# A scatter's wait moved ahead of the next scatter, and a one-hot table laid out with its tiles innermost

## The reference

```
sig = sigmoid(x @ Wg.T);  topk_idx = top_k(sig + e_bias, 6)         # 6 of 128 experts per token
topk_w = 2.5 * sig[topk_idx] / sum(sig[topk_idx])
# per expert a list of at most 192 (CAP) tokens with their weights
g, u = split(x[tokens_of_e] @ W_gate_up[e]);  y = (silu(g) * u) @ W_down[e] * weight
out = x_in;  out[tokens_of_e] += y;  out += (silu(x @ Wsg) * (x @ Wsu)) @ Wsd
```

## Time and profile before

| | |
|---|---|
| median of 3 runs | 946.81 us (944.99 to 950.73) |
| the profiled execution | 954.78 us, span 953.0 us |
| TensorE (PE) busy | 846.6 us, 89% |
| VectorE (DVE) busy | 750.6 us, 79% |
| ScalarE (ACT) busy | 343.4 us, 36% |
| GpSimd (POOL) busy | 308.2 us, 32% |
| last chain, by engine | DVE 41%, PE 28%, issue 11%, POOL 7%, DMA 7% |

### The profile page before, as it was taken

How to read it: one execution, slowest core, us unless ns; L and a number is a source line. 1 busy time by engine, 2 the same in 40 slices (tenths; PEclk the granted TensorE clock), 3 DMA queues, 4 the chain that set the end, 5 groups by cost and what they waited for, 6 DMA issues and landing times.

```text
span 953.0 us, 22207 instructions
## 1 busy us (share of the span) xinstructions
PE 846.6 (89%) x7603; PEld 766.5 (80%) x7603; DVE 750.6 (79%) x3738; ACT 343.4 (36%) x971; POOL 308.2 (32%) x350
## 2 busy tenths in 40 slices
PE   1787899899899899899899999998999999999993
PEld 1676688788798788788799999988878878878782
DVE  4256899999899899899999896988635666676662
ACT  0325554553553554544544435331100222122220
POOL 6021212412412312312313311031102556656564
PEclk8799999999999999999999999999986999999997
DMA  7410010110001001001101000001104455565541
GB/s 204 127 51 1 2 35 16 37 32 21 29 20 33 29 17 35 30 17 35 29 19 35 26 20 27 25 25 41 45 5 112 115 143 147 128 152 142 128 115 29
DMA packets 48663, 54.25 MB, mean 57 GB/s; under 512 B 8981, under 2 KB 41595, under 8 KB 48540
## 3 DMA queue, kind: packets, MB, share of 16 engines
q1 hardware_dynamic: 39372, 44.23, 16.3%
q0 software_dynamic: 6592, 7.28, 4.8%
q10 hardware_dynamic: 2608, 1.60, 0.7%
HBM read 42.40 MB, written 10.69 MB: 56 GB/s over the span
## 4 chain that ended last, share of the span: by engine, by line
DVE 41%; PE 28%; issue 11%; POOL 7%; DMA 7%; ACT 3%; SPq 2%; DVEq 0%; POOLq 0%; ACTq 0%
DVE b_arena L1497 10%; POOL b_arena L1758 4%; DMA out_rows<-b_hid,b_add_index 3%; POOL out_rows L1788 3%; DMA out_rows<-b_inner,b_add_index 3%; DVE b_top_a L1483 3%; PE p_big L685 3%; PE p_big L686 2%; DVE b_top_d L1483 2%; PE p_shared L830 2%; DVE b_top_c L1483 2%; PE p_shared L831 2%; DVE b_top_b L1483 2%; DVE b_rstd L1235 2%; PE p_small L866 2%
## 5 line engine op out<-in xcount | busy, mean ns | idle before, releaser
L1758 POOL DMA_INDIRECT b_arena<-x_rows,b_index x44 | 75.0, 1705 | 103.4 <-issue 66.3
L1541 DVE TENSOR_TENSOR b_arena<-b_iota_b,b_slot 128x1152 bf16<-128x1152 bf16 (+1 forms) x46 | 85.2, 1855 | 15.0 <-issue 15.0
L685 PE MATMUL p_big<-b_xT,b_ff1a 128*128 128x128 f32 x384 | 77.7, 285 | 1.4 <-ACT b_xT L1025 1.4
L686 PE MATMUL p_big<-b_xT,b_ff1b 128*128 128x128 f32 x384 | 76.9, 283 | 0.0
L1692 POOL TENSOR_TENSOR b_arena<-b_kY,b_mask_k 64x256 f32<-64x256 f32 x16 | 9.8, 611 | 204.8 <-ACT b_kY L1050 204.8
L1025 ACT COPY b_xT<-p_small 128x256 f32<-128x256 f32 (+1 forms) x97 | 35.5, 377 | 83.2 <-PE p_small L676 83.1
L1723 POOL TENSOR_TENSOR b_arena<-b_arena 128x768 f32<-128x768 f32 x16 | 27.0, 1690 | 117.6 <-DVE b_arena L1509 117.6
L685 PEld LDWEIGHTS p_big<-b_xT,b_ff1a 128*128 128x128 f32 x384 | 61.8, 200 | 2.5 <-ACT b_xT L1025 2.5
L686 PEld LDWEIGHTS p_big<-b_xT,b_ff1b 128*128 128x128 f32 x384 | 61.1, 200 | 0.0
L996 PE MATMUL p_big<-b_xeT,b_arena 128*116 128x192 f32 x320 | 60.1, 331 | 0.0
L719 PE MATMUL p_big<-b_arena,b_q_blk 128*128 128x256 f32 (+3 forms) x256 | 48.9, 334 | 12.4 <-ACT b_q_blk L1057 12.4
(11 more groups left out here) (367 smaller groups left out, 2589.6 us busy)
## 6 DMA issues: line engine op xcount, KB each, us to landing
b_arena<-in_w_gate_up SPq DMA_DIRECT2D x20, 464.0 KB
b_arena<-in_w_down SPq DMA_DIRECT2D x20, 336.0 KB
b_xp<-in_xp SPq DMA_DIRECT2D x16, 384.0 KB, 3.1
b_arena<-in_w_gate_up SPq DMA_DIRECT2D x40, 116.0 KB
xT_rows<-b_xmT SPq DMA_DIRECT2D x16, 128.0 KB, 1.8
b_xT_late<-xT_rows SPq DMA_DIRECT2D x16, 128.0 KB, 2.2
h_rows<-b_h SPq DMA_DIRECT2D x16, 96.0 KB, 1.6
x_rows<-b_xm SPq DMA_DIRECT2D x32, 48.0 KB, 2.0
```

Of the source, the lines that this page charges most:

```text
L685: mm(o, ff1a[:, c * 128:(c + 1) * 128], xTa[s][:], start=True, stop=False)
L686: last = mm(o, ff1b[:, c * 128:(c + 1) * 128], xTb[s][:], start=False, stop=True)
L1541: last = tt(hot[s][:, tiles, :], iota_b[:, None, :].to_broadcast([128, n, CAP]), slot[:, tiles, bass.ds(e, 1)].to_broadcast([128, n, CAP]) ...
L1758: G.indirect_dma_start(xg[s][:, h, :], None, x_rows[:, :], bass.IndirectOffsetOnAxis(index[s][:, h:h + 1], 0)).then_inc(S(f"gathered{s}"), 16)
```

## The change

`hot` is laid out with the 192 places outside and the tiles inside, 18 of them so that the number is even (`NTP`; the last is never used), and `slot` likewise with the experts outside and the tiles inside. The constants 1 to 192 are kept repeated 18 times (`iota_t`). All operands of the comparison then have innermost steps of one element. The comparison is made in two operations of 96 places, both behind the two silu products; TensorE takes the 96 weights of a load 18 elements apart. GpSimd counts `add_done` and issues the scatter after a wait for the scatter before, instead of waiting behind its own; the zero rows' two transfers move from SyncE's queue to GpSimd's and count on the semaphore `added`.

```
@@ -31,9 +31,9 @@
 DX = D + DB
 HS = CAP // 2
 NT = TILES + 1
+NTP = NT + 1
 DUMMY = T
 ROWS = T + CAP
-HOT_FIRST = 6
 AHEAD = 4
 LATE = 9
 LIST = E + 4
@@ -310,7 +310,7 @@
 
 
 SEMAPHORES = """
-    h3_kept0 h3_kept1 xT_kept0 xT_kept1 fetched0 fetched1 at0_T at1_T at0_aT at1_aT zero_rows x_stored
+    h3_kept0 h3_kept1 xT_kept0 xT_kept1 fetched0 fetched1 at0_T at1_T at0_aT at1_aT x_stored
     acc_stored0 acc_stored1 patch_mm xm_ready acc_ready c_xm_ready cls_x_stored  cls_acc_stored list_ready
     eup1 down_mm w_loaded0 w_loaded1 h0_ready h0_T ff0_xT ff0_up ff0_hid
     ff0_down y_ready y_T at0_xT at0_qk at0_v at0_k_sb at0_four at0_qk_sb at0_s
@@ -399,7 +399,7 @@
         cls_before_f = arena[1][0:B, 512:512 + TILES * 128]
         pat_before_f = arena[1][:, 0:TILES * B]
         iota_f = sb("iota_f", [128, CAP + 1])
-        iota_b = sb("iota_b", [128, CAP], bf16)
+        iota_t = sb("iota_t", [128, CAP, NTP], bf16)
         tok_f = sb("tok_f", [128, NT * 3])
         dummy_f = sb("dummy_f", [HS, 2])
         eval_f = sb("eval_f", [128, 2])
@@ -493,7 +493,7 @@
         chosen = sb("chosen", [128, NT, E], bf16)
         before_sum = sb("before_sum", [128, NT, E], bf16)
         wsplit = sb("wsplit", [128, NT, E + 1, 3], bf16)
-        slot = sb("slot", [128, NT, E + 1], bf16)
+        slot = sb("slot", [128, E + 1, NTP], bf16)
         counts, active_f = sb("counts", [128, 1]), sb("active_f", [128, 1])
         active = sb("active", [128, 1], bf16)
         rank, pick = sb("rank", [128, 1]), sb("pick", [128, LIST], bf16)
@@ -501,7 +501,7 @@
         n_pairs = sb("n_pairs", [1, 1])
 
 
-        hot, at = carve(0, 128, NT, CAP, dt=bf16)
+        hot, at = carve(0, 128, CAP, NTP, dt=bf16)
         rhs = two("rhs", [128, NT, 6], bf16)
         slot_a, slot_b = two("slot_a", [HS, 2]), two("slot_b", [HS, 2])
         slot_w, add_w = two("slot_w", [HS, 2]), two("add_w", [HS, 2])
@@ -607,8 +607,6 @@
                     sp.wait_ge(presets, 1)
                 for dst, src in group:
                     sp.dma_start(dst, src).then_inc(done, 16)
-            sp.dma_start(x_rows[T:ROWS, :].rearrange("(p r) d -> p (r d)", r=2), zrows[:]).then_inc(S("zero_rows"), 16)
-            sp.dma_start(out[T:ROWS, :].rearrange("(p r) d -> p (r d)", r=2), zrows[:, 0:2 * D]).then_inc(S("zero_rows"), 16)
 
             sp.sem_inc(S("x_stored"), 64)
 
@@ -924,7 +922,7 @@
                 pe.wait_ge(S("hot_ready"), v)
                 for h in range(2):
                     for t in range(NT):
-                        last = mm(lists_bank[s][0:HS, 400 + 6 * h:406 + 6 * h], hot[s][:, t, h * HS:(h + 1) * HS], rhs[s][:, t, :],
+                        last = mm(lists_bank[s][0:HS, 400 + 6 * h:406 + 6 * h], hot[s][:, h * HS:(h + 1) * HS, t], rhs[s][:, t, :],
                                   start=(t == 0), stop=(t == NT - 1))
                 last.then_inc(S("index_mm"), 1)
 
@@ -1407,7 +1405,7 @@
                 yield
                 V.tensor_copy(pat_before[:], pat_before_f)
                 V.tensor_copy(eval_b[:], eval_f[:])
-                V.tensor_copy(iota_b[:], iota_f[:, 1:CAP + 1])
+                V.tensor_copy(iota_t[:], iota_f[:, 1:CAP + 1].unsqueeze(2).to_broadcast([128, CAP, NTP]))
                 yield
                 for s in range(2):
                     V.tensor_copy(rhs[s][:, :, 0:3], tok_f[:].rearrange("p (t c) -> p t c", c=3))
@@ -1536,11 +1534,10 @@
 
                 e = dve.value_load(lists[0:1, bass.ds(j, 1)] if not isinstance(j, int) else lists[0:1, j:j + 1],
                                    min_val=0, max_val=E)
-                for tiles in (slice(0, HOT_FIRST), slice(HOT_FIRST, NT)):
-                    n = tiles.stop - tiles.start
-                    last = tt(hot[s][:, tiles, :], iota_b[:, None, :].to_broadcast([128, n, CAP]),
-                              slot[:, tiles, bass.ds(e, 1)].to_broadcast([128, n, CAP]), ALU.is_equal)
-                    if tiles.stop == NT:
+                for n in range(2):
+                    part = slice(n * HS, (n + 1) * HS)
+                    tt(hot[s][:, part, :], iota_t[:, part, :], slot[:, bass.ds(e, 1), :].to_broadcast([128, HS, NTP]), ALU.is_equal)
+                    if n:
                         V.tensor_copy(rhs[s][:, :, 3:6], wsplit[:, :, bass.ds(e, 1), :].squeeze(2)).then_inc(S("hot_ready"), 1)
                     yield
 
@@ -1567,7 +1564,7 @@
                 yield "slots_out"
                 for b in range(TILES // 4):
                     dve.wait_ge(S("slots_mm"), b + 1)
-                    stt(slot[:, 4 * b:4 * b + 4, 0:E], big[b // 2][:, b % 2, :].rearrange("p (t e) -> p t e", e=E), 1.0,
+                    stt(slot[:, 0:E, 4 * b:4 * b + 4].rearrange("p e t -> p t e"), big[b // 2][:, b % 2, :].rearrange("p (t e) -> p t e", e=E), 1.0,
                         chosen[:, 4 * b:4 * b + 4, :], ALU.add, ALU.mult).then_inc(S("slots_done"), 1)
                     yield
                 yield "rank"
@@ -1577,7 +1574,7 @@
                 yield
                 dve.wait_ge(step, noted("active_f", 1))
                 V.tensor_copy(active[:], active_f[:]).then_inc(S("active_ready"), 1)
-                stt(slot[0:B, TILES, 0:E], big[0][0:B, 0, 0:E], 1.0, chosen[0:B, TILES, :], ALU.add, ALU.mult)\
+                stt(slot[0:B, 0:E, TILES], big[0][0:B, 0, 0:E], 1.0, chosen[0:B, TILES, :], ALU.add, ALU.mult)\
                     .then_inc(S("slots_done"), 1)
                 yield "list"
                 dve.wait_ge(S("rank_mm"), 1)
@@ -1637,8 +1634,6 @@
                             ts(add_w[s][:], slot_w[s][:], 0.5, None, op0=ALU.mult).then_inc(S("kept"), 1)
                             dve.wait_ge(S("kept"), v)
                             indices_of(s, v + 2)
-                        if r == 0:
-                            next(slots)
                     run(slots)
 
 
@@ -1762,11 +1757,14 @@
                 yield "gather0"
                 pool.wait_ge(S("x_stored"), 64 * TILES + 64)
                 pool.wait_ge(S("cls_x_stored"), 32)
-                pool.wait_ge(S("zero_rows"), 32)
+                pool.wait_ge(S("added"), 32)
                 gather(0, 1)
                 yield "gather1"
                 gather(1, 2)
 
+            pool.wait_ge(presets, 1)
+            G.dma_start(x_rows[T:ROWS, :].rearrange("(p r) d -> p (r d)", r=2), zrows[:]).then_inc(S("added"), 16)
+            G.dma_start(out[T:ROWS, :].rearrange("(p r) d -> p (r d)", r=2), zrows[:, 0:2 * D]).then_inc(S("added"), 16)
             pool.wait_ge(S("pe_ready"), 1)
             pool.wait_ge(loads_tokenizer, 16 * len(tokenizer_loads))
             interleave("pool", *every(patches, positions, tokens, keys_queries, top_keys, routes), (TILES, route(1, 1, B, TILES)),
@@ -1774,7 +1772,7 @@
 
             pool.wait_ge(S("list_ready"), 1)
             n2 = pool.value_load(lists[0:1, 2 * LIST:2 * LIST + 1], min_val=1, max_val=E // 2)
-            pool.sem_inc(S("add_done"), 2)
+            pool.sem_inc(S("add_done"), 1)
             for s in range(2):
                 pool.wait_ge(S(f"acc_stored{s}"), 16 * TILES)
             pool.wait_ge(S("cls_acc_stored"), 16)
@@ -1783,12 +1781,12 @@
                     v = 2 * i + s + 1
                     gather(s, v + 2)
                     hold(pool, S("y_done"), v + 2)
-
+                    hold(pool, S("added"), 64 * i + 32 * s + 32)
+                    pool.sem_inc(S("add_done"), 1)
                     for h in range(2):
                         G.indirect_dma_start(out[:, :], bass.IndirectOffsetOnAxis(add_index[s][:, h:h + 1], 0),
                                              y[s][:, h, :], None, compute_op=ALU.add).then_inc(S("added"), 16)
-                    pool.wait_ge(S("added"), 64 * i + 32 * s + 32)
-                    pool.sem_inc(S("add_done"), 1)
+            pool.wait_ge(S("added"), 64 * n2 + 32)
             for s in range(2):
                 pool.wait_ge(S(f"gathered{s}"), 32 * n2 + 32)
 
```

32 lines of the change are left out of this document (16 added, 16 removed).

## The result

The changed kernel takes **1,079.04 us** (median of 4 runs, 1,078.62 to 1,079.29) against 946.29 us (944.99 to 950.73, 4 runs) for the kernel before: ratio 1.139, 95% interval 1.136 to 1.143. The forecast was 959 us, its range 931 to 970. Its sign was right and its size was a tenth of the real one.

A forecast was written before the change was run, and what follows sets the result against it. The prediction took GpSimd's wait for its own scatter to pace the expert loop. Its terms, -9.0 + 24.6 - 1.3 - 2.0 + 0.1 = +12.4 us, set on the 946.8 us median, gave 959 us, with an 8-in-10 range of 931 to 970.

The forecast's parts named there:

- weight loads, 22 groups: TensorE's table matmuls: weights 36 bytes apart load in 82 ns, not 45.6; +1.17 us per group, 21 groups, +24.6 us.
- granted clock of the loop: TensorE's clock in the expert loop: left unpriced; a fall below 1.0 was named as a way to be wrong.
- rounds without the wait: Expert loop: GpSimd's wait moved ahead of the next scatter, TensorE's rounds fall from 10.01 to 9.48 us, -9.0 us.
- first table: Ahead of the loop: a quicker first one-hot table removes TensorE's 1.36 us idle time, -1.3 us.
- the end: After the loop: the last scatter follows y (-1.4) and the last round's own wait goes (-0.5), -2.0 us.
- early work: Before the loop: copy of the replicated index table, 1.9 us, and moved zero-row transfers; +0.1 us, copy at most +2.
- upper bound: Spread weight loads on TensorE: at most 149 ns for 96 columns, from the loop's slowest load, +3.5 us per expert.
- break-even of 64 ns a load: TensorE's table loads: below 64 ns per load the first rival's side of the forecast holds.
- The two-element form: VectorE's table operations take two elements per step: 1.04 us each, 2.1 in place of 3.7 us per expert.
- The first rival: TensorE's table loads: spread weights load as fast as dense ones; -12.2, 934.6 us; chance 0.30.
- Rival 2: TensorE's table loads: slower still, near the upper bound; +61, about 1,008 us; chance 0.12.
- GpSimd, not the arithmetic, paces the loop: Expert loop: scatter follows scatter by about 10.01 us with a 3.1 us wait inside, holding TensorE above its 9.48 us.

The follow-up runs named there:

- pairs: Kernel before with each slot number stored twice, GpSimd's part of the change and both table operations behind the second silu product; 938.01 us, ratio 0.990.
- layout_alone: Changed kernel with the edits on GpSimd and the zero rows undone, so the table's layout alone; 1,079.20 us, ratio 1.124.
- step 4: Changed kernel with tiles innermost in groups of 2, weights of a load 4 bytes apart; 940.72 us, and 940.69 us (ratio 0.983) when run again.
- pairs_four_times: pairs with TensorE running each half's table product four times, 136 dense loads in place of 34; 1,112.85 us, ratio 1.166.
- wide: Changed kernel with the six columns moved through each of a group's 34 matmuls repeated ten times, 60 columns; 1,077.42 us, ratio 1.126.
- wait_alone: Kernel before with only GpSimd's part of the change (moved wait, zero rows on its queue), old table; 946.03 us, ratio 0.984.
- step 12: Changed kernel with tiles innermost in groups of 6, weights of a load 12 bytes apart; 1,036.07 us.
- step 8: Changed kernel with tiles innermost in groups of 4, weights of a load 8 bytes apart; 1,011.47 us.
- late_alone: Kernel before with one edit, both parts of the one-hot table behind the second silu product; 957.83 us, ratio 1.012.
- pairs_own_wait: pairs with GpSimd's wait behind its own scatter as in the kernel before; 938.32 us, ratio 0.978.

## Why the prediction was wrong

Where the 123.8 us between the two spans are, and what the forecast had:

| term | forecast | measured | from |
|---|---|---|---|
| weight loads, 22 groups | +24.6 | +99.1 | 20 x 4.58, and 4.13 + 3.37 ahead of the loop |
| granted clock of the loop | 0 | +40.5 | what is left: 38.1 in 19 rounds, 2.4 in the tail |
| rounds without the wait | -9.0 | -12.3 | 19 x 9.31 (pairs) against 189.15 |
| first table | -1.3 | -1.8 | first group at 716.77, before at 718.60 |
| the end | -2.0 | -1.8 | the tail of the kernel with the wait alone |
| early work | +0.1 | +0.1 | 5.76 us later at the loop's first L925, less 7.50 and -1.83 above |
| sum | +12.4 | +123.8 | |

The three small terms are weaker than they look. The first table group starts anywhere from 714.7 to 718.5 us in the kernels with spread weights, so of -1.8 us only the end of the 1.36 us of idle time ahead of it is shown. The tail of layout_alone, with GpSimd's old wait, is 28.7 us and that of the changed kernel 28.9, so the -1.8 us of the end, read from the kernel with the wait alone, can't be seen in this one. And the loop starts anywhere within 2 us for the same program (739.1 and 737.0 us in the two runs of step 4).

The 19 rounds from the first L925 (745.90) to the last (1,047.93) take 302.03 us. At 9.31 us, the round of "pairs", they would take 176.9; 19 x 4.58 for the loads makes 263.9, and the other 38.1 us, 2.0 a round, lie in L994, L999 and their neighbours at the 1.2 GHz level, as the round above shows. The tail behind it grew by 5.16 us: 4.58 for its own group, -1.8 for the end, and the rest to the clock.

**The step that failed first: the size of the load.** The forecast wrote "as if the read delivered four bytes at a time" and took 82 ns. Dense two-byte weights at 0.47 ns were read rightly. The 0.86 ns for float32 was the pace of columns that move, 128 of them in 0.11 us, and not of a load; that it fits was luck. The load's own pace shows in the kernel before where only 32 columns move behind 116 weights:

```profile
716.06 0.37 PE L831 MATMUL p_shared<-b_xT,b_wsgb 128*116 128x32 f32 x2
716.26 0.37 PE L830 MATMUL p_shared<-b_xT,b_wsua 128*116 128x32 f32 x2
```

Two loads go by in 0.20 us, 0.87 ns a weight, so the rate stands. But both rates are of dense loads, and 0.47 ns is a floor that a load with twice the lines hardly leaves (47.4 ns for 24 lines). A dense float32 load of 96 columns touches 24 lines, a load at 36 bytes 96. The group of 34 in 2.86 us, which the forecast took as agreeing with 82 ns, is one of dense loads at the 1.2 GHz level; in the same place the changed kernel's group takes 6.09 us, so that agreement was chance. The rows of the kernel before have no third step, and no two of them tell bytes from lines; the upper bound taken from a row, 149 ns, was also too low (180.3). It was another dense float32 load, and from dense rows one cannot bound a spread one. Scaled by the lines touched, 96 against 12, an upper estimate is 8 x 45.6 = 365 ns, and that holds the 180. The forecast also left the group at the lower level ahead of the loop free of cost; it cost 3.37 us. (Its break-even of 64 ns a load is 63 by its own terms; nothing rests on it.)

**The step that was left out: the clock.** "I leave the clock alone", and "if the clock of the loop falls below 1.0, which nothing here prices". It fell, and cost 40.5 us, a third of the loss. A sign stood in the rows: in the stretch 722 to 737 the clock was 0.51 with TensorE busy 14.9 of 15 us, around and behind the first table groups. What lowers it is shown only in part. It doesn't take spread loads (pairs_four_times), and it isn't few moving columns behind a load (wide), the GpSimd part (wait_alone stays at 1.00) or idle time (TensorE has none here). In all the runs whose group was 3 us or longer, spread or dense, the clock in the loop is 0.77 to 0.87; in the runs with 1.55 to 1.61 us and even rounds of 9.3 to 10.0 us it is 1.00. Between these it isn't monotonic: step 12 loses 1.6 us a round (13.88 against 9.31 + 3.01) and step 8, with a shorter group, 1.9 (12.70 against 9.31 + 1.54). The loss goes with the mean clock of those 19 rounds, 0.86 and 0.81, and not with the group. And late_alone dips once in three rounds with a short group. What sets how much of a round is spent at the lower level stays open.

**Right, point by point.** The two-element form: "1.04 us each", measured 1,046 to 1,060 ns over all 46. The copy of the replicated constants: 1.9 us forecast, 1.94 measured. The moved wait costs nothing. The wait ahead of the second half of the down projection is gone, and so is the idle time ahead of the first table group. GpSimd's gathers start on the index. The first rival, the load for free (934.6 us), has its likeness in "pairs", where the loads really are dense: 938.0 us. Rival 2 had the right direction, "the load is slower still", at 1,008 us; with 180 ns and a full clock its own sum would be 22 x 4.58 - 12.2, 88.6 us over the median before, about 1,035 us.

**Right for a reason that was half wrong.** "GpSimd, not the arithmetic, paces the loop" gave the right -9.0 against the profiled execution, but GpSimd did so only together with VectorE: late_alone ran two rounds in three at 9.69 us, and pairs_own_wait ran at 9.31, with GpSimd's wait untouched. Its round of 10.01 was made of the wait and of a gather that the table stretched from 0.96 to 2.15 us. Taking either off suffices. The -9.0 was also read from an execution of 954.8 us and set on a median of 946.8; if the quicker executions already have shorter rounds, which no profile shows, a part of it was counted that isn't there.

## What to carry to other kernels

A layout that gives the vector engine its fast form is paid for where another engine reads the same tile: count for the weights of a matmul the 16-byte lines that one load touches in a partition, here 1.9 ns each, before turning the innermost dimension over. A fast form asks for a pair of neighbours, not for a whole dimension; storing the one repeated operand twice gave the same speed (1.06 against 1.05 us for 1,728 elements) and left the table as it was. And when a change makes a group of short matmuls longer, leave room for the clock: here a third of the loss was work that hadn't changed and ran at half speed.

## What was not expected of the hardware

- A load of spread weights costs by lines and not by the clock: 179 ns at a granted clock of 0.50, 180 in the loop. A dense one costs 45.6 ns at 2.4 GHz and 80 at 1.2.
- Weights 4 bytes apart are nearly free: 47.4 against 45.6 ns. The changed kernel's idea works at that step: groups of two tiles gave 940.7 us, ratio 0.983, though VectorE then needs nine operations a table (352 ns each).
- The granted clock fell beside a TensorE that was busy all the time (286.15 of 286.15 us at 0.79), with dense loads as with spread ones, and with 60 moving columns as with 6.
- VectorE's table operation and GpSimd's descriptor generation slow one another: a gather takes 0.96 us alone and 2.0 to 3.0 beside the table in wait_alone, and VectorE's small copies take 0.30 us beside a scatter in the kernel before and 0.16 in wait_alone.
